# Attention and FFN kernel: two PSUM banks per read for the maxima, tanh and gate, the first weight quantised on GpSimd, and a new order of the steps

## What is computed

```python
def reference(x, ctx, W1, W2):          # x, ctx: (16, 256, 512)
    # attention: 8 groups of heads per 4 sequences; q = layernorm(x), k = v = ctx
    qk  = einsum('bdm,bdn->bmn', qh, kh) / sqrt(32)
    ret = einsum('bmn,bcn->bcm', softmax(qk), vh)
    x = x + ret
    # FFN: activations quantised to 8 bits per row, weights to -1, 0, 1
    n = layernorm(x)
    h = silu(bitlinear(n, W1))           # W1: (2048, 512)
    return x + bitlinear(h, W2)          # W2: (512, 2048)

def act_quant(x):    scale = 127 / max(max(abs(x), axis=-1), 1e-5); return round(x * scale) / scale
def weight_quant(w): scale = 1 / max(mean(abs(w)), 1e-5);           return clip(round(w * scale), -1, 1) / scale
```

## Time and profile before

| | |
|---|---|
| median of 3 runs | 797.79 us (797.62 to 798.24) |
| the profiled execution's own time | 797.01 us |
| its span, first to last instruction | 795.2 us |
| mean granted TensorE clock | 0.988 |
| busy PE, DVE, ACT, POOL | 716.8, 700.5, 633.4, 611.3 us |

### The profile page before, as it was taken

How to read it: one execution, slowest core, us unless ns; L and a number is a source line. 1 busy time by engine, 2 the same in 40 slices (tenths; PEclk the granted TensorE clock), 3 DMA queues, 4 the chain that set the end, 5 groups by cost and what they waited for, 6 DMA issues and landing times.

```text
span 795.2 us, 13866 instructions
## 1 busy us (share of the span) xinstructions
PE 716.8 (90%) x4324; PEld 279.0 (35%) x4324; DVE 700.5 (88%) x1596; ACT 633.4 (80%) x1017; POOL 611.3 (77%) x619
## 2 busy tenths in 40 slices
PE   0248899999999999999999999999999999999984
PEld 0012233333444333333333433333333434333332
DVE  1898799999999999999999999999999999998552
ACT  5757588888888888888888888888888888887852
POOL 2116678888898888888888988888888888887861
PEclk9999899999999999999999999999999999999996
DMA  8642333333333323333332343233333233320100
GB/s 295 220 106 81 80 80 108 107 94 100 81 88 107 103 83 96 107 107 106 89 90 85 100 108 95 81 106 107 108 95 99 81 87 108 79 68 16 67 27 13
DMA packets 53960, 76.66 MB, mean 96 GB/s; under 512 B 7808, under 2 KB 32384, under 8 KB 52864
## 3 DMA queue, kind: packets, MB, share of 16 engines
q1 hardware_dynamic: 53888, 75.79, 32.8%
HBM read 41.94 MB, written 8.39 MB: 63 GB/s over the span
## 4 chain that ended last, share of the span: by engine, by line
PE 73%; DVE 11%; ACT 9%; issue 4%; DMA 2%; POOL 1%; SPq 1%; POOLq 0%; ACTq 0%; DVEq 0%
PE pv L892 15%; PE bank_b L923 13%; PE st L872 11%; PE mxp L882 10%; PE bank_b L952 7%; PE dn L901 7%; PE bank_a L952 7%; DVE mx L707 5%; ACT probs L568 4%; ACT late L595 3%; DMA late<-w 2%; PE bank_a L911 2%; DVE late L828 1%; PE bank_a L929 1%; DVE late L826 1%
## 5 line engine op out<-in xcount | busy, mean ns | idle before, releaser
L568 ACT ACTIVATE probs<-st,sm 128x512 f32<-128x512 f32 x512 | 331.2, 688 | 53.7 <-PE st L872 27.4
L707 DVE TENSOR_REDUCE mx<-mxp 128x1 f32<-128x512 f32 x512 | 331.8, 679 | 20.3 <-PE mxp L882 19.4
L501 POOL TENSOR_TENSOR sums<-probs 128x512 f32<-128x512 f32 x256 | 328.4, 1303 | 23.5 <-ACT probs L568 23.4
L882 PE MATMUL mxp<-ks,qs 96*128 96x512 f16 x512 | 204.6, 401 | 33.2 <-DVE mx L707 27.1
L872 PE MATMUL st<-qs,ks 98*128 98x512 f16 x512 | 195.3, 392 | 1.0 <-ACT probs L568 0.9
L923 PE MATMUL bank_b<-w2t,late 128*128 128x512 f16 x512 | 128.6, 384 | 3.0 <-ACT late L595 3.0
L892 PE MATMUL pv<-probs,vt 128*32 128x512 f32 x1024 | 124.0, 602 | 0.0
L595 ACT ACTIVATE late<-bank_a 128x1024 f16<-128x1024 f16 x64 | 65.5, 1023 | 31.8 <-PE bank_a L911 31.6
L882 PEld LDWEIGHTS mxp<-ks,qs 96*128 96x128 f16 x512 | 53.2, 104 | 107.0 <-DVE mx L707 75.4
L781 DVE TENSOR_REDUCE hmx<-late 128x1 f32<-128x512 f32 x128 | 81.4, 678 | 0.0
L872 PEld LDWEIGHTS st<-qs,ks 98*128 98x128 f16 x512 | 48.0, 99 | 92.0 <-ACT probs L568 32.7
(11 more groups left out here) (77 smaller groups left out, 905.9 us busy)
## 6 DMA issues: line engine op xcount, KB each, us to landing
cs<-ctx SPq DMA_DIRECT2D x32, 256.0 KB, 3.1
xs<-x SPq DMA_DIRECT2D x32, 256.0 KB, 3.1
late<-w SPq DMA_DIRECT2D x8, 1024.0 KB, 6.8
ks<-kh SPq DMA_DIRECT2D x64, 128.0 KB, 3.5
qs<-qh SPq DMA_DIRECT2D x64, 128.0 KB, 3.2
vt<-values_t SPq DMA_DIRECT2D x32, 256.0 KB, 3.3
xr<-x SPq DMA_DIRECT2D x32, 256.0 KB, 3.4
out<-late SPq DMA_DIRECT2D x32, 256.0 KB, 2.2
```

The source lines that it names most:

```text
L501: pool.tensor_tensor(sums[:, pair, h, :], probs[:, 2 * pair, h, :], probs[:, 2 * pair + 1, h, :], ALU.add).then_inc(sum_done, 1)
L568: act.activation(probs[:, c, h, :], st[u % 2][:, :], ACT.Exp, scale=sm1[:, r, ESC:ESC + 1]).then_inc(exp_done, 1)
L707: dve.reduce_max(mx[:, slot.ring(off), NC * h + c:NC * h + c + 1], mxp[m % 2][:, :], axis=AX.X).then_inc(max_done, 1)
L882: pe.matmul(mxp[m % 2][:, :], qs[0:3 * DH, r, h, c * P:(c + 1) * P], ks[0:3 * DH, r, h, :], start=True, stop=True).then_inc(mx_done, 1)
```

## The change

- `mxp` becomes one tensor of two banks. `maxima` waits only before the even matmul, for the read of the whole pair before; `maximum` reads both banks in one instruction and writes two columns of `mx`. There are 8 reads a tile, where there were 16.
- `bank_b` and `bank_a` become the two halves of one tensor `banks`. `tanh` and `gate` each run over both at once (two a tile, where there were four), and `hidden_max` over half a row of `hu` (two, where there were four). `first` still has four groups; groups 2 and 3 wait for the first `gate`.
- The first weight is quantised by POOL (`weights_round`: multiply and round, then clamp), the second by DVE as before (`weights_clamp`).
- `PLAN`, `WEIGHTS` and `ORDER` have new numbers throughout.
- New waits in the first slots: `residual` of tile 0 waits for 5 conversions (it was all 8), `quantise` of tile 0 for 7, `hidden_evac` of tile 0 for 8.

```diff
-    maxima=[-22, -21, -20, -20, -19, -18, -17, -16, -13, -12, -11, -10, -10, -9, -8, -7],
+    maxima=[-22, -22, -20, -20, -18, -18, -15, -15, -14, -14, -11, -11, -10, -10, -9, -9],
-    max_read=[-21, -21, -20, -20, -19, -19, -18, -13, -13, -12, -12, -11, -10, -9, -8, -8],
+    max_read=[-21, -19, -17, -16, -12, -11, -9, -8],
...
-        mxp = [pb(f"mxp{k}", [P, D], f32) for k in range(2)]
+        mxp = pb("mxp", [P, 2, D], f32)
...
-        bank_a = pb("bank_a", [P, D], f32)
-        bank_b = pb("bank_b", [P, D], f32)
+        banks = pb("banks", [P, 2, D], f32)
+        bank_b, bank_a = banks[:, 0, :], banks[:, 1, :]
...
+            def weights_round(q):
+                part = wraw[:, q * F:(q + 1) * F]
+                pool.wait_ge(w_step, WS)
+                pool.tensor_scalar(part, part, wst[:, 0, 7:8], MAGIC, ALU.mult, ALU.add).then_inc(w_quant[0], 1)
+                pool.wait_ge(w_quant[0], 2 * q + 1)
+                pool.tensor_scalar(part, part, MAGIC + 1.0, MAGIC - 1.0, ALU.min, ALU.max).then_inc(w_quant[0], 1)
...
-            def tanh(slot, off, fc):
-                bank = (bank_b, bank_a)[fc % 2]
-                wait(act, f1_done, slot, FC, off, fc + 1)
-                wait(act, gate_done, slot, FC, off, fc - 1)
-                if fc == 0:
+            def tanh(slot, off, n):
+                wait(act, f1_done, slot, FC, off, 2 * n + 2)
+                wait(act, gate_done, slot, 2, off, n)
+                if n == 0:
                     wait(act, token_step, slot, 1, off, 1)
-                act.activation(th[:, fc % 2, :], bank[:, :], ACT.Tanh,
+                act.activation(th[:, :, :], banks[:, :, :], ACT.Tanh,
...
-            def maximum(slot, off, m):
-                c, h = divmod(m, TH)
-                wait(dve, mx_done, slot, UNITS, off, m + 1)
-                dve.reduce_max(mx[:, slot.ring(off), NC * h + c:NC * h + c + 1], mxp[m % 2][:, :], axis=AX.X).then_inc(max_done, 1)
+            def maximum(slot, off, n):
+                c, h = divmod(2 * n, TH)
+                wait(dve, mx_done, slot, UNITS, off, 2 * n + 2)
+                at = NC * h + c
+                dve.reduce_max(mx[:, slot.ring(off), at:at + NC + 1:NC], mxp[:, :, :], axis=AX.X).then_inc(max_done, 1)
...
-            def gate(slot, off, fc):
-                bank = (bank_b, bank_a)[fc % 2]
-                w = slice(fc * D, (fc + 1) * D)
-                if fc == 0:
+            def gate(slot, off, n):
+                w = slice(2 * n * D, 2 * (n + 1) * D)
+                if n == 0:
 
                     wait(dve, ht_done, slot, 2, off - 1, 2)
-                wait(dve, tanh_done, slot, FC, off, fc + 1)
-                dve.scalar_tensor_tensor(out=hu[:, w], in0=th[:, fc % 2, :], scalar=1.0, in1=bank[:, :],
+                wait(dve, tanh_done, slot, 2, off, n + 1)
+                dve.scalar_tensor_tensor(out=hu[:, w].rearrange("p (b d) -> p b d", d=D), in0=th[:, :, :], scalar=1.0, in1=banks[:, :, :],
                                          op0=ALU.add, op1=ALU.mult).then_inc(gate_done, 1)
...
-                wait(pe, max_done, slot, UNITS, off, m - 1)
-                pe.matmul(mxp[m % 2][:, :], qs[0:3 * DH, r, h, c * P:(c + 1) * P], ks[0:3 * DH, r, h, :],
+                if m % 2 == 0:
+                    wait(pe, max_done, slot, UNITS // 2, off, m // 2)
+                pe.matmul(mxp[:, m % 2, :], qs[0:3 * DH, r, h, c * P:(c + 1) * P], ks[0:3 * DH, r, h, :],
                           start=True, stop=True).then_inc(mx_done, 1)
```

More of the change, by code:

```diff
@@ L68 @@
+    quantise=[26],
     xqt=[27],
     xqt_evac=[26],
-    first=[28, 29, 30, 32],
-    tanh=[28, 29, 31, 31],
-    gate=[29, 30, 31, 31],
-    hidden_max=[30, 30, 31, 31],
-    hidden_scale=[31],
-    hidden_quantise=[29, 30],
-    ht=[37, 39],
-    ht_evac=[37, 39],
-    second=[39, 41, 41, 42],
-    finish=[44],
-    max_read=[-21, -21, -20, -20, -19, -19, -18, -13, -13, -12, -12, -11, -10, -9, -8, -8],
-    key_scale_b=[-17],
-    moments=[-33],
-    moments2=[23],
-    scale2_b=[25],
-    invert_b=[17],
@@ L86 @@
-    invert_c=[18],
-    hidden_scale_b=[32],
-    hidden_scale_c=[33],
-    hidden_scale_d=[34],
+    first=[28, 28, 31, 31],
+    tanh=[28, 31],
+    gate=[31, 32],
+    hidden_max=[31, 32],
+    hidden_scale=[34],
+    hidden_quantise=[34, 34],
+    ht=[35, 38],
+    ht_evac=[35, 38],
+    second=[37, 38, 40, 42],
+    finish=[48],
+    max_read=[-21, -19, -17, -16, -12, -11, -9, -8],
+    key_scale_b=[-2],
+    moments=[-43],
+    moments2=[23],
+    scale2_b=[26],
+    invert_b=[19],
+    invert_c=[20],
@@ L102 @@
 )
 WEIGHTS = dict(
[L107 to L124 removed]
+    load=[-34, -21, -21, -20, -12, 5, 10, 12],
@@ new lines @@
+    rows=[-42, -30, -23, 5],
+    abs=[-28, -27, -24, -21, -9, -1, 5, 7],
+    sum=[-23, 9],
+    quantise=[-21, -19, -1, 0, 9, 12, 15, 23],
+    convert=[-19, -8, -4, 1, 13, 17, 20, 24],
+)
+ORDER = {'pool': ['sums', 'quantise', 'hidden_quantise', 'xn', 'residual', 'ql', 'rstd2', 'finish', 'xn2', 'rstd',
+          'key_rsqrt'],
+ 'act': ['ct_evac', 'qh', 'rescale', 'kh', 'tanh', 'key_squares', 'quantise_act', 'ht_evac', 'xqt_evac'],
+ 'dve': ['stats_x', 'gate', 'scale2', 'moments', 'norm2b', 'invert', 'invert_c', 'max_read',
+          'hidden_scale', 'scale2_b', 'key_scale_b', 'hidden_scale_b', 'invert_b', 'hidden_scale_c',
+          'key_scale', 'ct_low', 'hidden_scale_d', 'attend', 'aggregate', 'hidden_max', 'norm2',
+          'moments2', 'kl', 'absmax2'],
+ 'pe': ['ct', 'maxima', 'values', 'ht', 'xqt', 'denominators', 'key_norm', 'second', 'first'],
+ 'sp': ['crow', 'stack_kh', 'load', 'xr', 'stack_kl', 'load_v', 'stack_qh', 'store', 'stack_ql']}
@@ L552, in run @@
                                 steps[name](slot, off, *number)
+                    for at, step, *which in weights:
+                        if at == UNITS * slot.b + u:
+                            step(*which)
             for b in range(-3, TILES + 4):
```

118 lines of the change are left out of this document (56 added, 62 removed).

## The result

The changed kernel takes 835.3 us (834.5 to 836.7), the kernel before, run beside it, 797.7; the ratio is 1.048, 95% interval 1.045 to 1.051. The forecast was 827, in a range of 792 to 850. The spans of the two profiled executions, 832.7 and 795.2 us, differ by 37.5 us, and the rest of this text accounts for these. Two executions that lay far above all others of the same kernel are left out everywhere: one of 11 of the kernel with `hidden_max` in two (1471.7 us) and one of 17 of the kernel before (815.9 us).

What follows compares the result with a forecast made beforehand. PE and DVE, both nearly full, were taken to bound the kernel, handing work over almost without a gap. From 797.0 us, start -11, slots +36 and end +6 gave 828, stated as 827 us, range 792 to 850.

Steps and rivals of the forecast that it cites:

- What the merging saves: DVE's wide reads: 0.07 us saved per merge, 12 a slot, 0.84 us of DVE work; 20.97 goes to 20.1.
- The price of 157 ns a merge: Skill page's fixed cost per DVE instruction; by it all 384 merges would save 60 us of DVE, by the rows 27.
- What the merging costs: Middle slots: with one pair of banks, PE and DVE wait for each other; slot 21.95 to 23.24 us, +36 us.
- The four waits: DVE idle per slot: 0.8 us between pairs 0 and 1, 1.0 and 0.4 before the gates, 0.8 before pair 7.
- the two waits of PE that it named: PE waits in a slot before the second eight matmuls of `first` and before pair 6 of the maxima.
- The start: Before the middle slots: first exponential near 49 us instead of 61.21, part lost in slots 0 and 1; -11 us.
- The end: Last two tiles: matmuls of `first`, tanh and gate run one after the other, 2.7 us more each; +6 us.
- A: Rival: faster, the chain shrinks below PE's own work of 21.2 us a slot; 765 us, chance 0.12.
- B: Rival: about even, better overlaps give a 22.3 us slot and the start gains 15; 797 us, chance 0.10.
- C: Rival: worse, waits held for hidden, as `ht` for `hidden_quantise`, join the chain; slot 24.3 us, 858 us, chance 0.08.
- the predicted chain: One slot's loop from pair 1 through `first`, tanh, gates, `hidden_max`, `attend`, reads and PE restarts to pair 1: 23.24 us.
- D: Rival: TensorE's granted clock, 1.00 in the slots, falls with the new idle gaps; chance within C's.

Runs made afterwards that it cites:

- `hidden_max` in two: Kernel before, with only `hidden_max` in two pieces of 1024 columns instead of four of 512: 796.9 us, ratio 1.0005.
- maxima-single kernel: Changed kernel with only the maxima read singly, one bank at a time; tanh, gate and `hidden_max` stay merged: 832.3 us, ratio 1.045.
- three lengthenings: `hidden_scale` moved ahead of the denominators' transpose in the change (854.3 us) and with maxima single (849.0); `kl` moved behind `hidden_scale` with all single (818.5).

## Why the prediction held, and where it did not

**What the merging saves**: right. 0.07 us a merge: a narrow pair in the maxima-single kernel takes 1.20 us of DVE (402.11 to 403.31 in its timeline), a wide read 1.13. In all these timelines the next instruction starts some 0.08 us before the recorded end of the last. The Trainium skill (VectorE: DVE Perf Modes, The DRAIN you can't avoid) has it start only when the pipe is empty, but adds that one that is not held starts earlier; the rows agree with the addition, which the prediction left out. The price of 157 ns a merge does not come out of the rows. The run with `hidden_max` in two, which did nothing else, does not decide this: what DVE saved there is waited for.

**What the merging costs**: right, 23.24 forecast, 23.14 measured. The four waits were given as 0.8, 1.0, 0.4 and 0.8 us and are 0.70, 0.69, 0.28 and 0.58. Some 0.08 us of three of the differences is counting: the forecast counts a wait from the step of a wide instruction, 1.14 us, the profile from its recorded end, 1.22. Before the first gate it is `kl`, 1.05 us long and not 0.74, which fills 0.3 us of the wait; that is also half of why DVE is busy for 20.67 us and not 20.1. The term was +36 and is +33.4. That the chain's stretch on DVE behind the second gate sets the slot is shown by three lengthenings (+0.58, +0.57 and +0.66 us), passed on as +0.57, +0.56 and +0.63. The rest of the chain is read from traces, and of the two waits of PE that it named one came (0.35 us before the second eight of `first`); before pair 6 PE has none. A statement that it implied, that the waits before the maxima carry half of the cost, is wrong: they are slack left over by the chain.

**The start**: the mechanism was half right and the size wrong; this is the mis-sized term, -11 forecast, -2.7 measured. The first exponential came at 49.67, as said (49). But slots 0 and 1 then took 53.4 us, where they took 44.6 before. The step that failed is "Of this 12 us some goes back in slots 0 and 1 ... I keep -11". The runs split it: the new order with GpSimd's part, unmerged, reaches slot 2 7.8 us sooner than before; the pair of banks for the maxima takes back 4.6 of that (102.62 against 97.98), tanh and gate 1.3 (99.31 against 97.98), both together 5.1. The maxima's lost buffer, worth nothing in the middle, is paid here, where two matmuls still take 1.03 us (0.60 from 76.97 us on) and DVE has long passes between the reads. Timeline of PE in the change's slot 0:

```profile
67.74 1.03 PE L902 MATMUL mxp<-ks,qs 96*128 96x512 f16 x2 [2.03 <-DVE mx L727]
...
72.52 1.03 PE L902 MATMUL mxp<-ks,qs 96*128 96x512 f16 x2 [2.89 <-DVE mx L727]
```

DVE was in passes over the second weight then, and with one pair of banks PE, the scores behind it and ACT stood still until the pass was over. Behind it, from 83 to 104 us, the granted clock is 0.76 (the lower of the two levels for part of the time), against 0.85 from 82 to 105 in the kernel before; what share of the 5.1 us that has was not tried.

**The end**: right, +6 forecast, +6.9 measured, and by the runs nearly all of it from tanh and gate (81.7 us from slot 30 on, 75.6 with them single).

**Rivals.** A and B did not come; the slot is neither near PE's 21.2 nor 22.3. C came in part: its wait exists (0.47 us before `ht`), and its way is as long as the predicted chain to within some 0.05 us, but no longer; the prediction had it hidden by 0.2 us. D: the clock in the slots is 1.00.

**The parts do not add up.** In the old order merging tanh and gate costs 93 us and merging the maxima 239; in the new one 30 and 3 to 4. The prediction worked out one chain in the new order and was not touched by this, but my expectations for the old order carried a price from one order to the other and missed by 61 and 239 us. They also had no term for the clock: from 200 to 700 us the granted clock is 1.00 in the kernel before and in all kernels of the new order, and 0.98 and 0.96 in the two mergings in the old one.

## What to carry to other kernels

Before two reads are merged into one, ask what their source was double-buffered for: the merge saves 0.07 us, and the lost overlap is the whole round trip of producer, reader and restart wherever a chain passes it. Follow one chain around the loop until it closes, and test it by lengthening one stretch of it: if the period grows by the same amount, that stretch is on a ring that sets it, while the places where an engine is idle may only be its slack. It does not show that the ring is the only one: here a second way was as long to within 0.05 us. A price measured in one hand-made order says little about another.
